# Routing weights and x are transposed in 32x32 blocks by VectorE instead of by TensorE, and layer norm 1 is folded into the query weights and the exponential

## The reference, cut to what matters

```
q = layernorm(x) @ Wq;  k, v = context @ Wk, context @ Wv
x = x + softmax(q k^T / 8) v @ Wo + bo
h = layernorm(x)
rw = gating(h)        # (256 tokens, 16 experts): normalised h @ sim - sigmoid(gates), relu, mask, softmax
q, k, v = sum over the experts e of rw[:, e] * (h @ q_proj[e], k_proj[e], v_proj[e])
a = causal_softmax(q k^T / 8) v
x = x + sum over e of (rw[:, e] * a) @ o_proj[e]
```

## Time and profile before

| | |
|---|---|
| median of 3 runs | 2549.08 us (2548.26 to 2549.45) |
| profiled execution | 2547.88 us, span 2546.1 us |
| mean granted TensorE clock | 0.989 |
| busy | PE 97%, DVE 83%, ACT 62%, POOL 43% |
| DMA | 441.48 MB, mean 173 GB/s |

### The profile page before, as it was taken

How to read it: one execution, slowest core, us unless ns; L and a number is a source line. 1 busy time by engine, 2 the same in 40 slices (tenths; PEclk the granted TensorE clock), 3 DMA queues, 4 the chain that set the end, 5 groups by cost and what they waited for, 6 DMA issues and landing times.

```text
span 2546.1 us, 54414 instructions
## 1 busy us (share of the span) xinstructions
PE 2477.4 (97%) x17308; PEld 2427.1 (95%) x17308; DVE 2124.1 (83%) x6126; ACT 1584.3 (62%) x5126; POOL 1104.3 (43%) x1741
## 2 busy tenths in 40 slices
PE   5799999999999999999999999999999999999997
PEld 5799999999999999999999999999999999999997
DVE  6788888888888888888888888888888888888885
ACT  6666666666666666666666666666666666666642
POOL 2244444444444444444444444444444444444442
PEclk8899999999999999999999999999999999999998
DMA  6765556465565556466565556465565556465531
GB/s 180 232 184 178 170 164 197 153 198 184 163 188 178 169 165 197 153 198 183 163 189 177 170 165 197 148 203 182 165 189 176 170 165 197 154 194 180 162 108 46
DMA packets 288070, 441.48 MB, mean 173 GB/s; under 512 B 20356, under 2 KB 199492, under 8 KB 279723
## 3 DMA queue, kind: packets, MB, share of 16 engines
q1 hardware_dynamic: 218155, 369.84, 44.6%
q10 hardware_dynamic: 69632, 68.17, 11.1%
HBM read 254.86 MB, written 181.83 MB: 172 GB/s over the span
## 4 chain that ended last, share of the span: by engine, by line
PE 81%; DVE 7%; POOL 5%; issue 3%; ACT 3%; DMA 0%; POOLq 0%; SPq 0%; DVEq 0%; ACTq 0%
PE bank_b L581 12%; PE bank_b L582 12%; PE bank_b L583 12%; PE bank_c L581 5%; PE bank_c L582 5%; PE bank_c L583 5%; PE bank_a L581 4%; PE bank_a L582 4%; PE bank_a L583 4%; PE bank_a L726 3%; PE bank_a L690 2%; PE bank_a L702 2%; DVE both L1433 2%; PE bank_a L691 1%; PE bank_a L665 1%
## 5 line engine op out<-in xcount | busy, mean ns | idle before, releaser
L1541 DVE SCALAR_TENSOR_TENSOR acc<-bank_b,rw,acc 128x192 f32<-128x192 f32 x1792 | 653.2, 408 | 108.9 <-PE bank_b L583 106.6
L581 PE MATMUL bank_b<-wqkv_hi,x2T_lo 128*128 128x384 f32 (+1 forms) x2048 | 721.3, 352 | 3.0 <-ACT acc L1142 1.6
L582 PE MATMUL bank_b<-wqkv_lo,x2T_hi 128*128 128x384 f32 (+1 forms) x2048 | 694.4, 339 | 0.0
L583 PE MATMUL bank_b<-wqkv_hi,x2T_hi 128*128 128x384 f32 (+1 forms) x2048 | 690.4, 337 | 0.0
L1915 POOL TENSOR_TENSOR mixs_lo<-mix,mixs_hi 128x512 fp32r<-128x512 f32 x254 | 378.2, 1520 | 164.5 <-ACT mixs_hi L1220 164.5
L1112 ACT ACTIVATE probs<-bank_a,s_max 128x77 f32<-128x77 f32 x1024 | 317.9, 331 | 202.3 <-DVE s_max L1471 202.3
L581 PEld LDWEIGHTS bank_b<-wqkv_hi,x2T_lo 128*128 128x128 f32 x2048 | 387.0, 189 | 5.4 <-ACT acc L1142 2.2
L582 PEld LDWEIGHTS bank_b<-wqkv_lo,x2T_hi 128*128 128x128 f32 x2048 | 387.5, 189 | 0.0
L583 PEld LDWEIGHTS bank_b<-wqkv_hi,x2T_hi 128*128 128x128 f32 x2048 | 385.5, 188 | 0.0
L1220 ACT ACTIVATE mixs_hi<-mix 128x512 fp32r<-128x512 f32 x256 | 159.8, 633 | 208.8 <-DVE mix L1582 208.8
L581 PE MATMUL bank_c<-wo_hi,mixs_lo 128*128 128x256 f32 x1000 | 281.2, 281 | 3.7 <-POOL mixs_lo L1915 3.7
(11 more groups left out here) (262 smaller groups left out, 6389.7 us busy)
## 6 DMA issues: line engine op xcount, KB each, us to landing
gq<-g_dram SPq DMA_DIRECT2D x63, 1232.0 KB, 5.7
rw_all<-rw_dram ACTq DMA_DIRECT2D x128, 512.0 KB, 6.8
uo<-u_dram SPq DMA_DIRECT2D x63, 1024.0 KB
g_dram<-draft SPq DMA_DIRECT2D x103, 462.0 KB
u_dram<-draft SPq DMA_DIRECT2D x127, 308.0 KB
g_dram<-mixs_lo SPq DMA_DIRECT2D x63, 462.0 KB
xt<-in_x_dram SPq DMA_DIRECT2D x64, 256.0 KB, 4.7
out_dram<-mix SPq DMA_DIRECT2D x62, 256.0 KB, 4.0
```

Source lines behind the costliest of these rows:

```text
L581: nc.tensor.matmul(dst, lhs[1], rhs[0], start=start, stop=False)
L582: nc.tensor.matmul(dst, lhs[0], rhs[1], start=False, stop=False)
L583: return nc.tensor.matmul(dst, lhs[0], rhs[0], start=False, stop=stop)
L1541: V.scalar_tensor_tensor(acc[:, t, k, :], src, rw[:, t, e:e + 1], acc[:, t, k, :], ALU.mult, ALU.add).then_inc(b_evac, 1)
```

## The change

- x comes twice from DRAM: as before for the statistics and the residual, and once more in four transfers a batch (`load_blocks`), laid out so that 32x32 block transposes by DVE (`a_blocks`) give x transposed. This x is not normalised. `a_xT` remains on ACT and DVE, at another place in the order, and reads SBUF (`x_cols`) where it read PSUM.
- the mean of layer norm 1 is taken out of the query weights in the opening (`query_weights`: each row's mean over the features is subtracted), and 1/sqrt(var) (with the score's 1/8 in it) becomes the scale of the exponential, a value per partition; DVE multiplies the maxima by it too. `ln1_b` falls away, and `minus` and `shift` of layer norm 1 with it.
- rw is kept as experts x token halves, transposed by DVE in blocks (`b_rwT`, after b_qkv 2), and stored by four transfers on SP's queue at the start of the next step (`store_rw`). `c_rT` falls away on TensorE and ACT.

```diff
 # SP
+            def load_blocks(n):
+                if n > 1:
+                    sp.wait_ge(pt_fill, at(3, n - 1, 2))
+                for k in range(4):
+                    sp.dma_start(x_blocks(n)[k * 32:(k + 1) * 32, :].rearrange("p (k c) -> p k c", k=TB),
+                                 x[n, :, :].rearrange("(k s) c -> s k c", s=32)[:, :, k * C // 4:(k + 1) * C // 4]).then_inc(xt_in[n % 2], 16)
+            def store_rw(n):
+                sp.wait_ge(rwT_ready, at(1, n, 0))
+                if n:
+                    sp.wait_ge(rw_all_in, 32 * n)
+                for k in range(4):
+                    tokens = slice(k * P // 4, (k + 1) * P // 4)
+                    sp.dma_start(rw_dram.rearrange("e (t x) -> (e t) x", t=NT)[:, tokens], rwT[tokens, :]).then_inc(rwT_out, 16)
             def step(i):
+                if on(i - 1):
+                    store_rw(i - 1)
...
                 turn(i, "E2")
+                if on(i + 2):
+                    load_blocks(i + 2)
                 turn(i, "E3")
 # TensorE
-            def a_xT(n):
-                pe.wait_ge(ln_done[0], at(NT, n, NT - 1))
-                for cc in range(CC):
-                    for t in range(NT):
-                        last = nc.tensor.transpose(bank_xt(n)[:, cc * T + t * P:cc * T + (t + 1) * P],
-                                                   xn[:, t, cc * P:(cc + 1) * P], ident[:, :])
-                last.then_inc(xt_fill, 1)
-            def c_rT(n):
-                if n:
-                    pe.wait_ge(aT2_ready, at(1, n - 1, 0))
-                pe.wait_ge(rw_ready, at(1, n, 0))
-                apart(pe)
-                for t in range(NT):
-                    last = nc.tensor.transpose(bank_rT[0:E, t * P:(t + 1) * P], rw[:, t, :], ident[:, :])
-                last.then_inc(rT_fill, 1)
 # ACT
             def a_xT(n):
                 act.wait_ge(xt_fill, at(1, n, 0))
-                nc.scalar.activation(xT[0][:, :, :].rearrange("p a b -> p (a b)"), bank_xt(n)[:, :], copy).then_inc(xt_hi, 1)
+                if n:
+                    act.wait_ge(s_fill, at(2 * NT, n - 1, 2 * NT - 1))
+                nc.scalar.activation(xT[0][:, :, :].rearrange("p a b -> p (a b)"), x_cols, copy).then_inc(xt_hi, 1)
...
                     last = nc.scalar.activation(probs[:, t, h * NC:(h + 1) * NC], bank_s(n, j)[:, k * NC:(k + 1) * NC], ACT.Exp,
-                                                bias=s_max[:, j, k:k + 1], accum_out=p_sum[:, half, 0, t, k:k + 1])
+                                                bias=s_max[:, j, k:k + 1], scale=pow_out[0][:, 0, t:t + 1], accum_out=p_sum[:, half, 0, t, k:k + 1])
...
-                do(before, c_rT)
...
-                do(nxt, ln1_b)
...
                 turn(i, "M1")
-                do(nxt, a_xT)
                 do(before, c_qk)
                 turn(i, "M2")
                 do(before, c_exp)
                 do(now, b_exp)
+                do(nxt, a_xT)
 # DVE
+            def a_blocks(n):
+                dve.wait_ge(xt_in[n % 2], 64 * (n // 2 + 1))
+                if n:
+                    dve.wait_ge(pt_fill, at(3, n - 1, 2))
+                V.transpose(x_cols.rearrange("p (a k s) -> p a k s", a=CC, k=TB),
+                            x_blocks(n).rearrange("p (k r a) -> p a k r", k=TB, a=CC)).then_inc(xt_fill, 1)
             def a_xT(n):
                 hi, lo = flat(xT, slice(None), slice(None), slice(None))
                 dve.wait_ge(xt_hi, at(1, n, 0))
-                V.tensor_tensor(lo, bank_xt(n)[:, :], hi.bitcast(F32), ALU.subtract).then_inc(xt_evac, 1)
+                V.tensor_tensor(lo, x_cols, hi.bitcast(F32), ALU.subtract).then_inc(xt_evac, 1)
...
                 V.tensor_reduce(s_max[:, j, :], bank_s(n, j)[:, 0:HB * NC].rearrange("p (a b) -> p a b", a=HB), AX.X, ALU.max,
-                                negate=True).then_inc(s_max_ready, 1)
+                                negate=True).then_inc(s_top, 1)
+                dve.wait_ge(ln_pow[0], at(1, n, 0))
+                dve.wait_ge(s_top, at(2 * NT, n, j))
+                V.tensor_scalar(s_max[:, j, :], s_max[:, j, :], pow_out[0][:, 0, j % 2:j % 2 + 1], None, ALU.mult).then_inc(s_max_ready, 1)
+            def b_rwT(n):
+                dve.wait_ge(rw_ready, at(1, n, 0))
+                if n:
+                    dve.wait_ge(rwT_out, 64 * n)
+                V.transpose(rwT[:, :], rw[:, :, :].rearrange("p e t -> p (e t)")).then_inc(rwT_ready, 1)
...
                 turn(i, "M1")
-                do(nxt, a_xT)
                 do(now, b_z, 0)
...
                 do(before, c_s)
+                do(nxt, a_blocks)
                 do(before, c_p)
...
                 do(now, b_wsum)
                 turn(i, "M2")
                 do(ahead, a_y)
+                do(nxt, a_xT)
                 turn(i, "M3")
                 do(before, c_pT)
                 do(now, b_qkv, 2)
+                do(now, b_rwT)
                 do(now, b_qkv, 3)
 # opening, query weights, on DVE
+                for k in range(HB):
+                    dve.wait_ge(wq_fill, k + 1)
+                    mean = wq_mean[:, 2 * k:2 * k + 2]
+                    V.tensor_reduce(mean, (banks_b[1:3] + banks_c)[k][:, :].rearrange("p (e c) -> p e c", e=2), AX.X, ALU.add,
+                                    negate=True).then_inc(wq_sum, 1)
+                    dve.wait_ge(wq_sum, k + 1)
+                    V.tensor_scalar(mean, mean, 1.0 / C, None, ALU.mult).then_inc(wq_mean_ready, 1)
```

More of the change, by code:

```diff
@@ L286, in xattn_moe_kernel @@
         xt_fill, xt_hi, xt_evac = sem("xt_fill"), sem("xt_hi"), sem("xt_evac")
+        xt_in, s_top = [sem(f"xt_in{k}") for k in range(2)], sem("s_top")
         s_fill = sem("s_fill")
@@ L606, in freed @@
                         return taken(*job(at_step, held))
-                return first_taken(*[held for held in OPENING if first_bank(*held) is bank_a(slot)][-1])
+                return first_taken(*[held for held in OPENING if held[0] != "xT" and first_bank(*held) is bank_a(slot)][-1])
             def first_taken(kind, f):
                 if kind == "xT":
-                    pe.wait_ge(xt_evac, at(1, f, 0))
-                elif kind == "s":
+                    return
+                if kind == "s":
                     pe.wait_ge(p_exp, at(2 * NT, f // (2 * NT), f % (2 * NT)))
@@ L869, in _ @@
                     j_u(0, f)
-                elif kind == "xT":
-                    a_xT(f)
                 elif kind == "s":
@@ L1164, in ln2_b @@
                     act.wait_ge(mix_lo, at(4, n - 2, 1))
-                ln_b(1, n, x2_tiles[n % 3], x2n)
+                act.wait_ge(ln2_shift, at(1, n, 0))
+                for t in range(NT):
+                    nc.scalar.activation(x2n[:, t, :], x2_tiles[n % 3][:, t, :], ACT.Identity, bias=shift[:, t:t + 1],
+                                         scale=pow_out[1][:, 0, t:t + 1]).then_inc(ln2_done, 1)
             def c_part(n, fill, dst, src):
@@ L1727, in _ @@
                 elif kind == "xT":
+                    a_blocks(f)
                     a_xT(f)
@@ L1779, in _ @@
             split_weights(12)
+            a_blocks(2)
+            b_qkv(0, 4)
             a_xT(2)
-            b_qkv(0, 4)
             turn(0, "M2")
```

110 lines of the change are left out of this document (49 added, 61 removed).

## The result

| | before | after |
|---|---|---|
| median | 2548.67 us (4 runs, 2546.77 to 2549.45) | 2641.24 us (4 runs, 2639.55 to 2645.19) |
| profiled span | 2546.1 us | 2643.4 us |
| TensorE's first `b_xT` (batch 0) | 79.7 us | 90.6 us |
| step of kind 0, 1, 2, mean | 38.05, 38.43, 38.13 us | 38.41, 41.95, 38.34 us |

The ratio is 1.0368 (95% interval 1.0353 to 1.0382). The prediction had slower with a chance of 0.72, but 2582 us, and a range up to 2608. Most of the mechanisms named were there, but the loads of the blocks, layer norm 1 and the opening were priced too low.

A forecast was written before the change was run, and what follows sets the result against it. TensorE, busy 97% of the span, was taken as the bound. Per three steps c_pv +1.41, weights' transposes -0.66 and PT2 +0.79 made +1.54; over 20.7 triples +32, with the opening +34: 2582 us, range 2545 to 2608.

The forecast's parts named there:

- Bound and place: TensorE bounds; savings count only from L1 to b_qkv 15; x's transposes gain 0, M2's wait growing to 0.6 us.
- Routing weights: Their transposes leave TensorE in the stretch without waits: -0.22 us a step, in full.
- Block transposes: DVE's 128x512 transposes of x between c_s and c_p: 0.69 us, hidden, bounds 0.5 and 1.4.
- The loads of the blocks: Four more SP issues a batch, after PT2, wanted at 1018.3: in time even at twice 4.7 us, taken as 0.
- DVE waiting for the blocks' DMA: A sign in the profile after that would show the prediction wrong.
- The low part of xT and c_pv: Subtraction moved on DVE ahead of c_pT delays c_pv by 0.35, 0.71 and 0.35 us: +1.41 per three steps.
- the rival: The port: POOL's xb gets ahead of a_xT, or block transposes hold up POOL's routing; 2601 or 2656 us, chance 0.10.
- Layer norm 1: Exponentials 0.1 us longer a pointer, DVE multiplications about 0.2 four times a batch; PT2 late in every third step.
- The sum +0.79 per three steps: Layer norm 1's delay of PT2, behind E2's evacuation, in every third step; 0 in the other two kinds.
- Opening: Reductions and small instructions on DVE before the first query weights, partly beside TensorE's transposes: +2 us, bounds 0 and 3.4.
- hidden exponentials: Rival: the pointer costs nothing or ACT catches up; triple +0.75 down to +0.3, 2551 to 2566 us, chance 0.22.

The follow-up runs named there:

- rw_only: Kernel before with only the routing weights transposed in blocks by DVE and stored by four SP transfers: 2538.92 us, ratio 0.9963.
- x_alone: repaired without layer norm 1's score scale, multiplications and query-weight centring, leaving both block transpositions: 2547.17 us, ratio 0.9995 to the kernel before.
- repaired: Kernel after with rw_behind, top_alone, xT_behind_pT and xb_waits joined, whole computation kept: 2568.21 us, ratio 1.0071 to the kernel before.
- top_alone: Kernel after without DVE's four multiplications of the row maxima, the exponential keeping its scale from memory: 2588.63 us, ratio 1.0148 to the kernel before.
- rw_behind: Kernel after with ACT's 1 MB of routing-weight loads issued behind the blocks of x, nothing left out: 2621.70 us, ratio 1.0285 to the kernel before.
- xb_waits: xT_behind_pT with POOL's sum of x and bias held until DVE's moved subtraction is done: 2636.94 us, ratio 1.0341 to the kernel before.
- e3: Not a run: E3 is a slot of the kernel's step, whose bank M2 uses.
- rw_once: Kernel after with the routing weights loaded for batch 0 alone, output wrong for the others: 2608.14 us, ratio 1.0229 to the kernel before.
- both_gone: Kernel after without layer norm 1's scale and multiplications in the scores, routing-weight loads behind the blocks: 2571.64 us, ratio 1.0085 to the kernel before.
- xT_behind_pT: Kernel after with DVE's subtraction for x's lower part moved behind that of the softmax's transpose: 2678.56 us, ratio 1.0507 to the kernel before.
- no_mean: Kernel after without centring the query weights, ScalarE copying each bank in one instruction: 2638.46 us, ratio 1.0355 to the kernel before.
- e2: Not a run: E2 is a slot of the kernel's step, whose bank PT2 takes.

## Why the prediction was wrong

| from the kernel before, 2549 | us |
|---|---|
| routing weights transposed by DVE (rw_only) | -10 |
| x's transposition moved, well placed (x_alone less rw_only) | +8 |
| layer norm 1 in query weights and exponential (repaired less x_alone) | +21 |
| multiplications, late blocks, port and order (after less repaired); undone alone they gave 53 (top_alone), 20 (rw_behind) and 4 (xb_waits) | +73 |

- *Bound and place.* Right. M2 waits 0.46 to 0.50 us for E3's evacuation, where near 0.6 was forecast, and x_alone's steps are no shorter than rw_only's: x's transposes pay nothing on TensorE.
- *Routing weights.* Right in sign, 0.15 instead of 0.22 us a step.
- *Block transposes.* Right: 0.709 us forecast at 0.69. The estimate from the Trainium skill's figure for bf16 ("VectorE: DVE Perf Modes", section "The three transpose paths"), 1.24 us, was not borne out.
- *The loads of the blocks.* **This step failed**: "at twice that they are still in time. Taken as 0." A landing of 7.1 us is even within twice the 4.7, but that counts each transfer from its own issue. These are issued just behind 1 MB of routing weights and two stores of u, with the DMA engines busy 0.97 of the time in one kind of step; the four issues alone take 5.7 us there, and the last block lands 11.5 us after the first issue, where the prediction's times (1009 to 1018.3) leave 9.3. With the 1 MB behind them the kernel is 20 us shorter (rw_behind), without it 33 (rw_once). "DVE waiting for the blocks' DMA" was named as what would show the prediction wrong, without a rival of its own.
- *The low part of xT and c_pv.* Right in kind, too dear by two fifths. I had 0.35, 0.71 and 0.35; by c_pv's start after `b_xT`, kinds 0 and 2 show a shift of 0.21, kind 1 (once the blocks are in time) 0.6, together 1.02; by the steps of both_gone and x_alone it is 1.09. The subtraction starts ahead of POOL's sum and pays nothing for the port; POOL does. That the port decides by order was the rival, and xT_behind_pT is that rival made to happen: +37 us.
- *Layer norm 1.* **This step failed too, in size.** The exponential's 0.1 us a pointer was good: 86 ns. It stands near the 93 ns that the Trainium skill gives in "ScalarE: Activation LUTs", section "What ACT_TABLE_LOAD costs". "About 0.2 four times a batch" was not: each multiplication brings 0.1 us of wait with it, the fourth takes 0.87 us beside POOL, and I counted only two of the four into ACT's chain, so that its fourth group waits for DVE again. The sum +0.79 per three steps was 2.34, measured with the blocks in time; 0.33 of it is in the two kinds of step for which I had 0. With the multiplications gone too, the pointer alone costs 0.83 (115.14 in repaired less 114.31 in x_alone), as much as I had for both.
- *Opening.* +2, bounds 0 to 3.4, for 10.9 us in the first `b_xT` and 4.2 in the interval after it. **This step failed as well.** Of the 10.9, centring the query weights is 6.3 (no_mean), and x_alone still has 82.3 us for 79.7. I had the reductions in part beside TensorE's transposes, and they are not; ScalarE's evacuations, eight instructions for four, and VectorE's come after them, and the first product with the query weights is 3.6 us later. How much of the rest is the granted clock, 0.70 for 0.85 up to the first `b_xT`, and how the second interval's 4.2 us come about, stays open.

With these terms put right, 2582 + 20 for the blocks + 34 for layer norm 1 (50 for 16) + 13 for the opening (15 for 2) + 4 for the routing weights (0.46 for 0.66, 20.3 times) - 8 for c_pv (1.02 for 1.41) make 2645, against 2641 measured. Some 4 us of the opening stand in this twice, in the 50 and in the 15. Three of the terms are differences from runs of the kernel after itself, so the sum tells that little is counted twice or missed, and not why each term is as large as it is.

Three of the prediction's own figures are off by its own premises, and none of them changes the forecast: its sum gives 2583 (2549.08 + 34) and not 2582; a block transpose of 1.24 us would cost 0.53 in every third step (1.24 less the first 0.71), 11 us and not 6; and the lower end of the hidden exponentials, +0.3 three steps with the opening's 2, is 2557 and not 2551.

## What to carry to other kernels

A transfer's landing time holds for the moment in the step at which it was measured, and several transfers in a row land one issue after the other. Before a new load is costed at nothing, list what every queue has in flight at its issue, in each kind of step, the other engines' queues included. When a small dependent instruction is put into an in-order chain, count it in every round, and look at what the neighbour on its memory port does at that moment. When a load is moved out of the way, look whether its own reader now waits. And a factor that softmax cancels needn't be applied, as long as the exponentials stay within range.

## What the hardware showed

- SP's issue of a 64 KB transfer takes 0.32 us at best and up to 3.2 us (up to 2.99 in the step read, with the DMA engines busy for 0.97 of the 9 us around it); what stands behind it on SP goes out only then (1219.84).
- A DVE multiplication of 128x4 elements with its factor in SBUF: 0.23 us, and 0.87 when a POOL tensor_tensor of 1.22 us is under way.
- Two SBUF inputs on DVE beside such a POOL instruction: 0.68 us if DVE starts first, and POOL's then goes from 1.30 to 1.59; 1.44 if POOL had started 0.4 us before, with POOL's at 1.30.
- TensorE's granted clock fell to the lower level (a mean of 0.96 over the step) in 6 of 17 long steps of the kernel after, each 1.2 us longer than the others, and in none where the blocks were in time (rw_once, rw_behind).
